# Block 2's last steps in another order, and seven kept tiles with the token rows summed through TensorE

## The reference

```
x = x + xcond(cond, ctx, layernorm(x))      # 3 rounds of:
    q = ln(slots) @ wq + bq;  logits = k . q / 16
    attn = softmax over the slots + 1e-8;  attn /= its sum over the context rows
    slots = attn @ v @ wu + bu + slots
    slots = gelu(ln(slots) @ w1 + b1) @ w2 + b2 + slots
    slots = ln(slots + cond)
x = x + ffn(layernorm(x)):
    scores = sigmoid(h @ gate_w.T)
    best 4 of 8 groups by their two best (scores + bias), best 8 experts in them
    weights = scores of these 8, divided by their sum, times 2.5
    routed = sum over the 8 of  weight * down_e( silu(gate_e(h)) * up_e(h) )
    out = routed + shared expert(h)
```

## Time and profile before

| | |
|---|---|
| median of 3 runs | 615.25 us (614.66 to 616.51) |
| profiled execution | 616.87 us, span of its instructions 615.6 us |
| mean granted clock of TensorE | 0.975 of full speed |
| busy: PE, DVE, ACT, POOL | 563.7, 411.4, 372.2, 363.9 us |
| chain that ended last, share by engine | PE 70%, DVE 10%, POOL 6%, ACT 6%, DMA 5%, issue 3% |
| DMA | 119.69 MB, mean 194 GB/s |

### The profile page before, as it was taken

One profiled execution on the slowest core, in us unless ns is written; L12 is line 12 of the kernel. 1 busy time (PEld: TensorE's weight loads), 2 busy tenths in 40 slices (PEclk: granted clock), 3 DMA queues, 4 the chain that ended last, 5 costly groups with the idle time before them and its releaser, 6 DMA issues.

```text
span 615.6 us, 11543 instructions
## 1 busy us (share of the span) xinstructions
PE 563.7 (92%) x2669; PEld 419.9 (68%) x2669; DVE 411.4 (67%) x1587; ACT 372.2 (60%) x993; POOL 363.9 (59%) x414
## 2 busy tenths in 40 slices
PE   3989989889998898698998999999999999999995
PEld 2656557655766455455656888888888888888774
DVE  6965675986768987648776444445444444698778
ACT  1858888768776755552611666566566666676660
POOL 4334233622143377886777777777777777777730
PEclk9979999999999799899799999999999999999998
DMA  7999300000000023239364999876666667999956
GB/s 259 394 397 380 120 0 2 0 1 0 2 0 1 14 94 118 97 118 341 119 223 179 314 315 338 284 224 205 202 207 201 210 199 216 353 412 397 413 184 244
DMA packets 62063, 119.69 MB, mean 194 GB/s; under 512 B 8667, under 2 KB 45583, under 8 KB 59951
## 3 DMA queue, kind: packets, MB, share of 16 engines
q1 hardware_dynamic: 48079, 77.63, 37.5%
q0 software_dynamic: 13488, 41.04, 17.7%
q10 hardware_dynamic: 432, 0.29, 0.2%
HBM read 61.29 MB, written 57.64 MB: 193 GB/s over the span
## 4 chain that ended last, share of the span: by engine, by line
PE 70%; DVE 10%; POOL 6%; ACT 6%; DMA 5%; issue 3%; SPq 0%; DVEq 0%; POOLq 0%; ACTq 0%
PE ps L2027 20%; PE ps L2047 10%; PE ps L1689 6%; PE ps L1663 6%; PE ps L1678 5%; PE ps L1886 5%; PE ps L1702 5%; POOL xrows L609 4%; DMA hat<-yrows 3%; PE ps L2040 3%; PE ps L1649 2%; PE ps L1781 2%; PE ps L1787 2%; DVE tokrow L749 2%; DMA xs<-in_x 1%
## 5 line engine op out<-in xcount | busy, mean ns | idle before, releaser
L2027 PE MATMUL ps<-arena,mats 128*128 x636 | 164.2, 381 | 0.3 <-issue 0.3
L609 POOL DMA_INDIRECT xrows<-tokrow,place_of x128 | 125.8, 983 | 42.9 <-issue 37.2
L1274 DVE TENSOR_TENSOR mats<-ps,mats 128x128 f32<-128x128 f32 x159 | 46.3, 291 | 104.1 <-ACT mats L1460 99.8
L2027 PEld LDWEIGHTS ps<-arena,mats 128*128 128x128 f32 x636 | 108.5, 190 | 9.3 <-issue 0.8
L2047 PE MATMUL ps<-arena,mats 128*128 x318 | 95.7, 383 | 1.0 <-DVE mats L1281 1.0
L1460 ACT ACTIVATE mats<-ps 128x128 f32<-128x128 f32 x159 | 44.1, 277 | 57.0 <-PE ps L2027 57.0
L1453 ACT COPY mats<-ps 128x256 f32<-128x256 f32 x159 | 57.9, 364 | 11.8 <-PE ps L1886 11.8
L1402 ACT ACTIVATE hat<-tokrow,shift,rstd 128x256 f32<-128x256 f32 x96 | 49.7, 590 | 14.1 <-POOL shift L540 14.1
L1394 ACT ACTIVATE hat<-tokrow,total 128x256 f32<-128x256 f32 x96 | 47.5, 499 | 17.0 <-DVE tokrow L814 10.3
L2047 PEld LDWEIGHTS ps<-arena,mats 128*128 128x128 f32 x318 | 48.0, 191 | 13.5 <-issue 1.9
L545 POOL TENSOR_SCALAR var_eps<-variance 128x4 f32<-128x4 f32 x24 | 6.4, 266 | 83.5 <-ACT hat L1394 83.2
(11 more groups left out here) (239 smaller groups left out, 1136.4 us busy)
## 6 DMA issues: line engine op xcount, KB each, us to landing
hat<-xrows SPq DMA_DIRECT2D x81, 160.0 KB
rows<-xrows SPq DMA_DIRECT2D x78, 160.0 KB
arena<-in_experts SPq DMA_DIRECT2D x4, 1920.0 KB, 18.9
xrows<-padrow SPq DMA_DIRECT2D x32, 160.0 KB
hat<-yrows SPq DMA_DIRECT2D x5, 1024.0 KB, 9.0
tokrow<-yrows SPq DMA_DIRECT2D x5, 1024.0 KB, 9.6
hatT<-yrows SPq DMA_DIRECT2D x5, 1024.0 KB, 9.3
xrows<-padrow SPq DMA_DIRECT2D x1, 4960.0 KB
```

The source lines that it names most:

```text
L609: gp.indirect_dma_start(out=xrows[:, :], out_offset=bass.IndirectOffsetOnAxis(ap=place_of[:, g, k:k + 1], axis=0), in_=tokrow[:, g, :], in ...
L2027: mm = te.matmul(bank(6 + u)[:, 0:2 * I], turned_row[u][:, dc * P:(dc + 1) * P], arena[:, dc * D:(E - 1) * WCOL + (dc + 1) * D][:, bass.ds ...
```

## The change

Four edits. The number of kept tiles goes from 6 to 7; the place of the seventh matrix is in `shared`, at columns whose results in `ybuf` have been scattered before (hence a new wait in `spread_tokens(6)`). The first three of a group are no longer a multiple of three from the first kept tile, so `find_tokens` is called for k = 0 as well as at each new group.

TensorE now starts the four accumulations with `ident` times the token rows `xs`, and signals `combined` once behind these four and once behind all. VectorE's last sums are written over `xs` by the third add (once `combined` >= 1), and the fourth add, `add_to_token`, goes for these four token tiles; `add_kept` waits for 2.

On POOL `from_squares(2, 5)` goes ahead of `dispatch(0, 13)`, and `from_tokens(2)` ahead of `dispatch(1, 7)` and `from_moments(3, 4)`. On VectorE `add_tokens(2)` goes ahead of `residual(3, 2)`, `slot_moments(3)` and `shared_product(1, 1)`. On TensorE `transpose_block(2, 6)` goes ahead of `shared_down(1)`.

```diff
--- before.py
+++ after.py
@@ -65,7 +65,7 @@
 YLATE = 130
 YHELD = 20
 
-KEPT = 6
+KEPT = 7
 
 SHIFT_AT = 116
 WHOLE = 8388608.0
@@ -256,7 +256,10 @@
         last_back = place(arena, 0, TOPK, D)
 
         of_token = [part(hatT[1][:, :, :], k * TQ * P, TQ, P) for k in range(4)]
-        of_token += [part(tokrow[:, :, :], k * TQ * P, TQ, P) for k in range(KEPT - 4)]
+        of_token += [part(tokrow[:, :, :], k * TQ * P, TQ, P) for k in range(2)]
+
+        of_token += [place(shared, 2 * D, TQ, P)]
+        OF_SHARED = (YLATE - YHELD + 31) // YGROUP
         into_token = part(mats[:, 4, :, :], GROUP * E * 3, GROUP)
         token_of = part(mats[:, 4, :, :], GROUP * (E * 3 + 1), GROUP)
         local = part(mats[:, 4, :, :], GROUP * (E * 3 + 2), GROUP, TQ)
@@ -671,8 +674,8 @@
             dispatch(0, 10)
             dispatch(0, 11)
             dispatch(0, 12)
+            from_squares(2, 5)
             dispatch(0, 13)
-            from_squares(2, 5)
             dispatch(0, 14)
             from_squares(3, 5)
             dispatch(0, 15)
@@ -684,9 +687,9 @@
             dispatch(1, 4)
             dispatch(1, 5)
             dispatch(1, 6)
+            from_tokens(2)
+            dispatch(1, 7)
             from_moments(3, 4)
-            dispatch(1, 7)
-            from_tokens(2)
             dispatch(1, 8)
             dispatch(1, 9)
             from_tokens(3)
@@ -1212,10 +1215,10 @@
             shared_product(1, 0)
             condition(3, 2)
             norm_slots(2, 2)
+            add_tokens(2)
             residual(3, 2)
             slot_moments(3)
             shared_product(1, 1)
-            add_tokens(2)
             norm_slots(3, 2)
             add_tokens(3)
             add_shared(1)
@@ -1295,8 +1298,10 @@
 
             def spread_tokens(k):
 
+                if k == 6:
+                    ve.wait_ge(scattered[OF_SHARED % YGROUPS], 16 * YGROUP * (OF_SHARED // YGROUPS + 1))
                 ve.tensor_tensor(of_token[k], tile_iota[:, 0:P].rearrange("p (o c) -> p o c", o=1).to_broadcast([P, TQ, P]),
-                                 local[:, k % GROUP, :].rearrange("p (t o) -> p t o", o=1).to_broadcast([P, TQ, P]),
+                                 local[:, (TILES - KEPT + k) % GROUP, :].rearrange("p (t o) -> p t o", o=1).to_broadcast([P, TQ, P]),
                                  ALU.is_equal).then_inc(token_known, 1)
 
             def add_half(y, half):
@@ -1327,7 +1332,7 @@
             def add_kept(half):
 
                 if half == 0:
-                    ve.wait_ge(combined, 1)
+                    ve.wait_ge(combined, 2)
                 g = EARLY_SUMS + 2 * half
                 at = (4 + 2 * half) * BANK
                 ve.tensor_tensor(xs[:, g:g + 2, :], ps[:, at:at + 2 * BANK].rearrange("p (b c) -> p b c", b=2)[:, :, 0:D],
@@ -1357,7 +1362,7 @@
                         last_of_sums(g)
                 k = n - (TILES - KEPT) - 1
                 if 0 <= k < KEPT:
-                    if k % GROUP == 0:
+                    if k == 0 or (TILES - KEPT + k) % GROUP == 0:
                         find_tokens((TILES - KEPT + k) // GROUP)
                     spread_tokens(k)
 
@@ -1371,8 +1376,10 @@
                 seq.add()
                 step(add_half(y, 1))
                 step(add_quarters(y))
-                step(add_last(y))
-                step(add_to_token(g, y))
+
+                if g == EARLY_SUMS:
+                    ve.wait_ge(combined, 1)
+                step(ve.tensor_tensor(xs[:, g, :], y[:, 0, :], y[:, 1, :], ALU.add))
             for half in range(2):
                 add_kept(half)
 
@@ -1996,8 +2003,8 @@
             hidden(3, 2)
             project_back(3, 2)
             shared_gate_up(1, 1)
+            transpose_block(2, 2 * ROUNDS, slots)
             shared_down(1)
-            transpose_block(2, 2 * ROUNDS, slots)
             gate_logits(2)
             shared_gate_up(2, 0)
             transpose_block(3, 2 * ROUNDS, slots)
@@ -2071,12 +2078,16 @@
 
             te.wait_ge(row_copied, TILES)
             te.wait_ge(act_ready, TILES)
+
+            for t in range(TQ):
+                mm = te.matmul(bank(4 + t)[:, 0:D], ident[:, :], xs[:, EARLY_SUMS + t, :], start=True, stop=False)
+            mm.then_inc(combined, 1)
             for k in range(KEPT):
                 n = TILES - KEPT + k
                 te.wait_ge(token_known, k + 1)
                 te.wait_ge(y_ready, n + 1)
                 for t in range(TQ):
-                    mm = te.matmul(bank(4 + t)[:, 0:D], of_token[k][:, t, :], ybuf[y_place(n)], start=k == 0,
+                    mm = te.matmul(bank(4 + t)[:, 0:D], of_token[k][:, t, :], ybuf[y_place(n)], start=False,
                                    stop=k == KEPT - 1)
             mm.then_inc(combined, 1)
 
```

## The result

The changed kernel took 621.96 us (median of 4 runs, 620.13 to 623.61) beside 614.95 us for the kernel before (4 runs, 614.26 to 616.51): ratio 1.0101, 95% interval 1.007 to 1.0133. It is slower, and above the range on record. Three further comparisons of the same two kernels gave 1.0040 [1.0003, 1.0078], 1.0067 [1.0035, 1.01] and 1.0077 [1.0054, 1.01]. In all four the interval lies above 1; the size is 0.4 to 1%. These ratios leave out executions that took over 1.5% longer than the fastest of their kernel, which in the second and third comparison drops 9 and 10 of the 35 executions of the kernel before, and none and one of the changed kernel's 12. By the medians of all executions the four are 1.0114, 1.0017, 1.0065 and 1.0080, so the second shows little by itself. Taken with 614.95 us, the three later ratios would be 617.4, 619.1 and 619.7 us.

A forecast was written before the change was run, and what follows sets the result against it. The chain of waits put 70% of the span on TensorE. Tail +1.5 us (0.36 + 1.1) less upstream gain 0.7 gave +0.8 us: 616.05 us against a median of 615.25, range 613.1 to 618.1.

The forecast's parts named there:

- Last scatter 1.27 us earlier: End, POOL: tile 151's scatter becomes the last, so the wait for all scatters ends 1.27 us earlier.
- VectorE's sums 1.9 us shorter: End, VectorE: each of four token tiles loses its last add, 4 × 0.48 = 1.9 us.
- TensorE's tail +3.51: End, TensorE: 24 matmuls behind the loop become 32, adding 3.51 us.
- TensorE becomes the bound, +0.36: End: TensorE's sums finish at 612.33 against 611.97 now, so savings on VectorE and POOL are only cover.
- Selection work +1.1: Tile loop's end, VectorE: one more `find_tokens` and `spread_tokens` ahead of `product(153)` delay the loop 1.1 us, bounds 0 and 1.22.
- from_squares(2, 5), 0: Block 2, POOL: the earlier call waits 1.8 us for ScalarE; taken as worth 0, ends -1.1 and +0.73.
- Block 2's chain, a gain of 0.7 at `rank(2)`: Block 2: `rank(2)` starts 3.1 us earlier, less 2.4 for the clock's fall, a gain of 0.7 us.
- Upstream gain 0.7 reaches the end: From `rank(2)` through the tile loop: block 2's 0.7 us is subtracted in full from the kernel's total.
- the prediction's own tail sum, +1.5 us: Loop's end and tail: 0.36 for TensorE's later end plus 1.1 for selection work, +1.5 us, slower.
- slower by one more stretch at half clock: Rival, chance 0.16: clock falls under block 2's `project_back(2, 2)`, ending later than 270.5; total +2.3, 617.6 us.
- the clock stays up: Rival, chance 0.22: no clock fall near `rank(2)`, 2.2 to 3.1 us arrive, total -0.7 to -1.6, 614.4 us.
- VectorE stays the last: Rival, chance 0.12: selection work hides and the clock stays up, TensorE's sums end near VectorE's; 2.8 us less, 612.4.

The follow-up runs named there:

- order_only: Kernel before with only block 2's new order, 6 kept tiles and the old sums: 615.09 us, ratio 0.9999 [0.9971, 1.0026].
- tail_only: Kernel before with seven kept tiles and TensorE's identity products, old order of block 2: 617.85 us, ratio 1.0039 [1.0017, 1.0061].
- order_late_squares: order_only with `from_squares(2, 5)` back at its old place behind `dispatch(0, 13)`: 720.72 us, ratio to the kernel before 1.0025 [0.998, 1.007].
- kept7_only: Kernel before with only the seventh kept tile, VectorE's old sums and old order: 616.73 us, ratio 1.0016 [0.9994, 1.0039].

## Why the prediction was wrong

The sign of the sum was right (+0.8), as was the bound of the tail; the size was too small. By its steps:

- *Last scatter 1.27 us earlier.* Tile 151's scatter was issued 7.92 us before the end of the loop (601.10 - 593.18); the last one of before stood 7.75 before (598.29 - 590.54). The issue gained only 0.17 us against the loop, but the first load back reached VectorE 0.5 us ahead of the loop's end (600.57), where before it came 1.7 behind it (600.03). So the wait fell by 2.3 us, more than forecast. It is cover, because VectorE isn't the bound now.
- *VectorE's sums 1.9 us shorter.* From the first to the last own sum: 11.21 us (600.57 to 611.78), 11.85 before (600.03 to 611.88). The four adds went, but 0.50 for TensorE's identity products and 0.75 for a load back came. The stall of at most 0.5 for the products was right.
- *TensorE's tail +3.51.* 13.97 - 10.53 = 3.44: right, and VectorE's wait (about 3 us forecast) is 3.43.
- *TensorE becomes the bound, +0.36.* Right at 615 us: 0.44 in the pair of traces, 0.96 against order_only's. At 720 us it is 2.1 to 2.7, since the wait for the first load back is not there. The forecast read the VectorE side from one execution; the two other traces with six kept tiles at 615 us bear it out.
- *Selection work +1.1.* 1.2 to 1.3 in three kernels, at or just above its upper bound of 1.22; right.
- *from_squares(2, 5), 0.* POOL waited 2.04 us (1.8 forecast), block 3's shift made ScalarE wait 2.46. Set beside tail_only, whose transposes before it ran at the same time, `project_back(2, 2)` starts at 267.29 instead of 266.32: a loss of 1.0 us at that place, near the forecast's worse end (-1.1), and not 0. order_late_squares couldn't tell its worth from nothing.
- *Block 2's chain, a gain of 0.7 at `rank(2)`.* Against the kernel before it came 2.7 us sooner after the attends (50.94 to 48.24), but tail_only with the old order shows 48.94. What the new order gives is 0.7: the number of the forecast. Its parts were not as forecast: the clock's fall lay at 290.8 and lasted 3.2 us, not in 297 to 308, and it lengthened `shared_down(1)` from 3.72 to 5.31, 1.6 us, where I had put 2.4; the 1.0 us of the squares isn't in the forecast. So the right number is in part luck.
- *Upstream gain 0.7 reaches the end.* **This step failed.** The sum takes the tile loop as lasting the same whatever comes before, and has no term for it. The changed kernel's loop took 245.40 us from the first product to tile 148's, against 243.95 before and 244.14 in tail_only. Beside tail_only, which differs by the order alone, it was 0.6 us ahead at the first product (336.35 against 336.99), 0.6 behind at tile 148 (581.75 against 581.13) and 0.8 behind at the final adds (615.21 against 614.42). Instead of -0.7 the stretches before the selection work gave +1.4.

Why the loop took longer stays open. The waits of 1.14 and 1.00 us for loads back stand in this trace, and POOL was late, but POOL was as late in order_only (its first scatter in the loop at 346.91, 346.73 in the changed kernel) and that loop took 245.21; kept7_only's, with the old order and POOL only 0.5 us behind before's, took 246.79.

By the traces: 0 + 1.4 + 1.3 + 0.4 = +3.2 (rounded), against 0.8 on record; the missing gain of 0.7 and the 1.4 in the loop are 2.1 of the 2.4 that are missing. The rest of the 7.0 in the medians is that the one trace is the fastest of four and the other above its median (1.8 and 1.9 us). That is no cause: what made the medians differ by 7.0 isn't shown by the traces.

The halves at 615 us, 0.9999 and 1.0039, add to 1.0038, and the prediction's own tail sum, +1.5 us, lies inside the interval of tail_only (+1.0 to +3.7 us). So the tail edits are a shown cause of a loss of about 0.4%. The first measurement of the whole, 1.0101, lies above the halves by 0.0063, 3.9 us, more than the 0.0048 that their intervals allow. Four runs are few, but I can't show that this is chance: **open** is where those 3.9 us went. An interaction of seventh tile and order was tested and not supported.

The rival "slower by one more stretch at half clock" was nearest in time (617.6) and is not what happened in the trace: `project_back(2, 2)` took its usual 3.72 us at 267.29. It ended at 271.0, beyond the 270.5 that I had set, which comes from the 2.5 us that the execution was late; and the clock's fall at 290.8 was the shorter one. The Trainium skill, "TensorE: Matmul & The Clock Gate", section "HAM oscillation — how this bites in real kernels", describes bursts of matmuls that waits put back to half clock one after another. The traces agree in part. In the changed kernel a wait of 2.60 us before 288.40 was followed by 3.2 us at 0.50, and in order_only the same wait by none. The rivals on the fast side, "the clock stays up" and "VectorE stays the last", are refuted for this execution by the fall at 290.8 and by VectorE's wait of 3.43 us.

## What to carry to other kernels

Moving work to the engine that bounds the program pays only as far as the other engine's lateness reaches, and that lateness is a difference of two large times: read it in several executions before it is taken as cover. Here it held at 615 us in three traces and was gone at 720 us. A gain early in a program arrives at its end only if every stretch between lasts the same, and a long loop doesn't: here it varied by 2.8 us between six traces, four times the gain. Compare a trace with one that differs by a single edit and came to the place equally late; beside the kernel before, most of what was regained looked like the edit's. Where executions spread over 5 us or more, a gain of 1 us needs the parts measured apart, many times, more than it needs another look at one trace.

## What the runs showed of the hardware

**The same program in 615 and in 720 us.** Nothing in the kernel differs between them, and one chip showed both: 614.72 us in one set of comparisons and 722.62 in a later one. The stretches before 240 us and the tile loop's later part are alike. Between 240 and 480 us engines stand still for long, in part with nothing that the profile names as the reason. TensorE's windows of the two executions of the unchanged kernel, 60 us at full speed in the first, 80 us in the second:

```profile
400.00:460.00 60.00, 59.51 (x329) 49.97 (x328) 28.12 (x121) 36.75 (x110) 45.67 (x48) 1.00 0.68 211
```

```profile
400.00:480.00 80.00, 48.85 (x188) 36.16 (x187) 16.59 (x71) 22.12 (x65) 49.94 (x52) 0.73 0.55 186
```

VectorE's two largest waits there, in the longer execution; the second has no releaser in the profile.

```profile
DVE mats L1274 <- ACT mats L1460: 37.9, 12, 10.2
DVE mats L1274 <- issue: 23.2, 7, 9.5
```

The columns are total us, times, longest. What the wait of 9.5 us is, the runs don't say. Ratios measured in this condition are of the same size as at 615 us, but waits of one engine for another are not: VectorE's for the first late load, with six kept tiles, is 1.97 to 2.50 us in three traces at 615 us and none to 0.40 in the six at 720 us.

**The clock falls in other places from one execution to the next.** Attends at 44 us took 9.13 us instead of 7.60, by clock 0.76 against 0.91 in the same window, in code that no edit touches. In block 2 the kernels with the new order had their second fall behind 2.60 us of idleness in one execution (290.8, for 3.2 us) and behind 2.47 us before `rank(2)` in another (304.8, for 6.8 us), with none behind the 2.60. The 35 runs of the unchanged kernel spread over 6.9 us (612.15 to 619.01), those of order_only over 9.5 us.
